# Layer 1 of a two-layer R-GCN: SP loads one tile of the even step row by row, ACT one tile of the odd step

## What is computed

```python
def _rgcn_conv(x, src, dst, edge_type, W_r, W_root, b):
    seg = dst * r + edge_type
    msg = x[src]
    agg = segment_sum(msg, seg, n * r).reshape(n, r, d)
    cnt = segment_sum(ones, seg, n * r).reshape(n, r, 1)
    mean = agg / maximum(cnt, 1.0)
    return einsum('nrd,rdk->nk', mean, W_r) + x @ W_root + b
...
h = maximum(_layernorm(x), 0); x = x + _L0_gnn_ref(h, src, dst)
h = maximum(_layernorm(x), 0)
for l in range(2):
    h = relu(_rgcn_conv(h, ...)) + relu(h @ res_W[l] + res_b[l])
x = x + h
```

## Time and profile before

| | |
|---|---|
| runs | 10280.56, 10290.72, 10291.77 us; median 10290.72 us |
| profiled execution | 10278.55 us, of which the span of its instructions is 10276.7 us |
| layer 1, first to last gather | 2367.31 to 6330.91 us |
| layer 2, first gather | 6362.22 us |
| busy share of the span | POOL 73%, DVE 52%, PE 44%, PE weight loads 32%, ACT 22% |
| mean granted TensorE clock | 0.65 of full speed |

### The profile page before, as it was taken

The page is one execution under the profiler, slowest core; times in us unless marked ns, Lnnn a source line. Parts: engine busy times, 40 slices in busy tenths (PEclk is TensorE's granted clock), DMA queues, the critical chain, the costliest instruction groups (busy, mean ns, idle before and its releaser), DMA issues.

```text
span 10276.7 us, 178961 instructions
## 1 busy us (share of the span) xinstructions
PE 4477.1 (44%) x38502; PEld 3253.0 (32%) x38601; DVE 5355.0 (52%) x19831; ACT 2249.7 (22%) x5858; POOL 7548.9 (73%) x8087
## 2 busy tenths in 40 slices
PE   4488888884444444444444443222222222222222
PEld 3366666662222222222222222222222222222222
DVE  9866666666667767767767765222222222222222
ACT  7855555551111111111111111000000000000000
POOL 6667777766777777777777776777777777777777
PEclk8899999996666666666666666555555555555555
DMA  3244444445444444444444443111111111111112
GB/s 89 63 139 149 147 147 147 148 136 171 146 149 143 145 149 143 145 148 139 149 148 141 147 148 120 30 29 29 29 29 29 29 29 29 29 29 29 29 29 41
DMA packets 534216, 1014.18 MB, mean 99 GB/s; under 512 B 242660, under 2 KB 289268, under 8 KB 532964
## 3 DMA queue, kind: packets, MB, share of 16 engines
q1 hardware_dynamic: 256500, 746.14, 20.0%
q0 software_dynamic: 251296, 259.66, 13.1%
q10 hardware_dynamic: 25872, 2.47, 0.3%
HBM read 557.66 MB, written 454.36 MB: 98 GB/s over the span
## 4 chain that ended last, share of the span: by engine, by line
POOL 64%; issue 24%; PE 5%; DVE 5%; ACT 1%; DMA 1%; POOLq 0%; DVEq 0%; SPq 0%; ACTq 0%
POOL rows L895 35%; POOL w_raw L895 28%; DVE ystage L1643 2%; PE block_ps L1399 1%; PE y_ps L1313 1%; ACT scr L1048 1%; PE y_ps L1391 1%; DVE onehot L1678 1%; PE sums_ps L1364 1%; DVE w_parts L1826 0%; DVE w_room L1826 0%; PE signs_ps L1313 0%; DMA rows<-h_table,idx_st 0%; DMA y_table<-ystage 0%; POOLq L496 0%
## 5 line engine op out<-in xcount | busy, mean ns | idle before, releaser
L895 POOL DMA_INDIRECT rows<-y_table,idx_st x3136 | 2961.6, 944 | 1036.6 <-issue 1036.6
L895 POOL DMA_INDIRECT w_raw<-y_table,idx_st x3163 | 2986.7, 944 | 964.9 <-issue 964.9
L1749 DVE TENSOR_SCALAR rr<-rr 128x64 f32<-128x64 f32 x198 | 41.3, 209 | 4073.5 <-PE block_ps L1341 4073.5
L1510 PE MATMUL sums_ps<-onehot,rows 128*64 128x64 f32 x6468 | 755.2, 313 | 2632.6 <-DMA rows<-y_table,idx_st 2557.9
L1510 PE MATMUL sums_ps<-w_raw 128*64 128x64 f32 x6424 | 751.4, 314 | 2542.0 <-DMA w_raw<-y_table,idx_st 2505.4
L895 POOL DMA_INDIRECT rows<-h_table,idx_st x1386 | 1323.9, 955 | 554.2 <-issue 435.3
L1510 PEld LDWEIGHTS sums_ps<-onehot,rows 128*64 128x64 f32 x6468 | 702.7, 222 | 2712.5 <-DMA rows<-y_table,idx_st 1607.7
L1510 PEld LDWEIGHTS sums_ps<-w_raw 128*64 128x64 f32 x6424 | 704.9, 224 | 2615.7 <-issue 2094.1
L999 ACT ACTIVATE idx_st<-edges 128x11 int32 (+1 forms) x714 | 140.7, 211 | 5545.0 <-PE sums_ps L1510 3061.9
L1688 DVE TENSOR_SCALAR_CACHE_REDUCE w_parts<-edges,step_key 128x384 bf16<-128x384 f32 x1568 | 850.7, 605 | 15.6 <-DVE step_key L1668 15.6
L1292 PE MATMUL y_ps<-scr,hT 128*128 128x512 bf16 (+1 forms) x2574 | 728.3, 428 | 111.7 <-ACT hT L1009 93.7
(11 more groups left out here) (238 smaller groups left out, 7495.9 us busy)
## 6 DMA issues: line engine op xcount, KB each, us to landing
y_table<-ystage SPq DMA_DIRECT2D x396, 768.0 KB
edges<-key_row SPq DMA_DIRECT2D x198, 832.0 KB
rows<-y_table SPq DMA_DIRECT2D x9408, 0.2 KB
y_table<-ystage SPq DMA_DIRECT2D x198, 608.0 KB
w_raw<-y_table ACTq DMA_DIRECT2D x6272, 0.2 KB
w_parts<-key_row SPq DMA_DIRECT2D x99, 832.0 KB
w_raw<-y_table,idx_st POOLq DMA_INDIRECT x3163
rows<-y_table,idx_st POOLq DMA_INDIRECT x3136, 2.5
```

What stands on the lines that cost most here:

```text
L895: pool.indirect_dma_start(out=rows_of(l, u)[:, j, k, 0:D], out_offset=None, in_=table, in_offset=bass.IndirectOffsetOnAxis(ap=idx_of(l, u, ...
L1510: ins = nc.tensor.matmul(sums_ps[u][0:width, c:c + W], rows_of(l, u)[:, j, k, 0:width], onehot_of(l, u)[:, j, k, :], start=False, stop=False)
```

## The change

In layer 1 the odd step's tile 10 is taken from POOL as well. SP now loads the whole tile of the even step, ACT the whole tile of the odd step, each four batches a step. ACT's batches stand where layer 2 has them, so that in layer 1 one lies after each `stage` of the first third, one after each of the three groups of evictions; ACT also loads the row numbers of its own tile and places them at the end of the even step.

```diff
-    ROW_LAYER = 2
-    ACT_ROWS = 32
...
         def by_rows(l, u):
-            return l == ROW_LAYER or l == 1 and u == 0
+            return l >= 1
...
-                    per_step = 32 if l == 1 else ROW_HALF
-                    load_rows(sp, mybir.EngineType.SP, l, 0, 0, 2 * per_step)
+                    load_rows(sp, mybir.EngineType.SP, l, 0, 0, P)
...
                         def next_rows(n):
                             if more:
-                                load_rows(sp, mybir.EngineType.SP, l, 0, u * per_step + n * (per_step // 2), per_step // 2)
+                                load_rows(sp, mybir.EngineType.SP, l, 0, u * ROW_HALF + n * (ROW_HALF // 2), ROW_HALF // 2)
...
-                    if l == 1:
...
-                        wait_alone(act, row_placed[0], loads)
-                        load_rows(act, mybir.EngineType.Activation, l, 0, P - 2 * ACT_ROWS, 2 * ACT_ROWS)
...
+                    load_row_idx(act, 1, 0, 1)
+                    place_rows(1, loads)
+                    wait_alone(act, row_placed[1], loads)
+                    load_rows(act, mybir.EngineType.Activation, l, 1, 0, ROW_HALF)
...
                         def next_rows(n):
-                            if l == ROW_LAYER and (more or u == 0):
+                            if more or u == 0:
                                 load_rows(act, mybir.EngineType.Activation, l, 1,
                                           (1 - u) * ROW_HALF + n * ROW_BATCH, ROW_BATCH)
-
-                        def shared_rows(n):
-                            if l == 1 and more:
-                                load_rows(act, mybir.EngineType.Activation, l, 0,
-                                          P - 2 * ACT_ROWS + u * ACT_ROWS + n * ROW_BATCH, ROW_BATCH)
...
                         if u == 0 and more:
                             place_rows(0, i + loads + 1)
-                            if l == ROW_LAYER:
-                                load_row_idx(act, 1, i + 1, 1)
-                            else:
-                                wait_alone(act, row_placed[0], i + loads + 1)
+                            load_row_idx(act, 1, i + 1, 1)
                         stage_ahead(0)
                         next_rows(0)
-                        shared_rows(0)
...
-                        shared_rows(1)
...
                         next_rows(3)
-                        if l == ROW_LAYER and u == 0 and more:
-                            place_rows(1, i + 2)
-                            wait_alone(act, row_placed[1], i + 2)
+                        if u == 0 and more:
+                            place_rows(1, i + loads + 1)
+                            wait_alone(act, row_placed[1], i + loads + 1)
```

More of the change, by code:

```diff
@@ L430, in gnn_kernel @@
         gathered = [[[sem(f"gathered{l}{u}{j}") for j in range(J)] for u in range(2)] for l in range(3)]
-        rows_landed = [None] + [[sem(f"rows_landed{l}{n}") for n in range(l)] for l in (1, 2)]
+        rows_landed = [None, [sem("rows_landed10"), sums_saved[1]], [sem(f"rows_landed2{n}") for n in range(2)]]
         row_idx_loaded = [sem(f"row_idx_loaded{n}") for n in range(2)]
@@ L1131, in _ @@
                     place_rows(0, loads)
-                    if l == 1:
-                        for slot in range(2):
-                            n = YG * NBK
-                            act.wait_ge(y_saved[l - 1][slot], 16 * ((n + 1 - slot) // 2 + 1))
-                        wait_alone(act, row_placed[0], loads)
-                        load_rows(act, mybir.EngineType.Activation, l, 0, P - 2 * ACT_ROWS, 2 * ACT_ROWS)
-                    if l == ROW_LAYER:
[L1139 to L1145, removed]
+                    for slot in range(2):
+                        n = YG * NBK
+                        act.wait_ge(y_saved[l - 1][slot], 16 * ((n + 1 - slot) // 2 + 1))
+                    load_row_idx(act, 1, 0, 1)
+                    place_rows(1, loads)
+                    wait_alone(act, row_placed[1], loads)
+                    load_rows(act, mybir.EngineType.Activation, l, 1, 0, ROW_HALF)
                     def act_step(i, u, last=False):
```

## The result

The changed kernel took 10618.46 us (median of 4 runs, 10603.67 to 10623.23), the kernel before 10291.24 beside it: a ratio of 1.0318, 95% interval 1.030 to 1.0336, some 327 us slower. The forecast was 10258 us and its range ended at 10380.

A forecast was written before the change was run, and what follows sets the result against it. POOL's gathers were taken to bound layer 1 at 81.2 us a pair; afterwards ACT and SP's 37.6 + 42.4 = 80.0 nearly tied POOL's 79.9, giving -32 us with the layer's ends: 10258 us, range 10222 to 10380.

The forecast's parts named there:

- What bounds the kernel, and what the change removes: POOL's back-to-back gathers, 1.249 us each, bound layer 1; 49 fewer remove 61.2 us, a pair going from 81.2 to 79.9.
- Even to odd, 37.6 us: ACT's loop, even to odd step in layer 1: 30.15 us seen in layer 2 plus 7.4 of evictions.
- the mark: ACT's `stage` of the second third, from which step intervals are measured; step 0 reaches it at 65.9 us.
- Odd to even, 42.4 us: Longer chain through SP, odd to even step in layer 1: 12.9 + 15.9 + 1.15 + 4.56 + 7.86 us.
- SP's jump: Rival, chance 0.09: SP's jump back fetches code, 3.3 us more odd to even, pair 83.3 us, +126 us, 10417 us.
- The landing, 4.56: Odd to even: ACT can place the next pair's row numbers 4.56 us after SP issues their load.
- ACT's own jump back lies under this wait.: Odd to even: ACT's last batch ends at 26.9 us, placing can start at 34.5, so its jump is covered.
- Slow register loads: Rival, chance 0.21: ACT's loads slow while saves and keys move; pair 82.6 us, 92 us longer, 10383 us.
- POOL keeps the bound: Rival, chance 0.23: pair of ACT and SP below 79.4 us; gain 61 us, 10229 us.
- near tie: Likeliest case, chance 0.26: pair of ACT and SP between 79.4 and 80.2 us, -61 to -21 us.
- no change: Rival, chance 0.21: pair of 80.2 to 81.1 us; gain given back at the layer's end.
- The start and the end of the layer.: Layer 1: step 0's mark at 65.9 us, last `hT` copy at 3936.9 after POOL's first gather, today 3969.4.

The follow-up runs named there:

- last rows first: Changed kernel plus early row numbers, shifted SP/ACT loops, groups 0 and 1 evicted together, some PE zero products, even-step last ACT batch before group 2's eviction: 10231.83 us, 0.9954.
- SP's loops elsewhere: Changed kernel with 30 already met waits on SP ahead of layer 1, so SP's loops lie at another place of the program: ratio 1.0250.
- the numbers early: Changed kernel, but in layer 1 SP loads the even tile's row numbers a pair ahead: 10445 us, ratio 1.0162.
- ACT's part alone: Changed kernel, but only ACT's odd-step tile is loaded by ACT; the even step's tile comes from POOL, SP loads no rows in layer 1: ratio 1.0223.

## Why the prediction was wrong, point by point

What failed is the sum for the loops of ACT and SP: 80.0 us a pair were forecast, 87.4 measured, 4.0 too little from even to odd and 3.4 from odd to even.

**What bounds the kernel, and what the change removes.** Right: a layer of 64 gathers a pair takes 80.0 us a pair (64 x 1.250, forecast 79.9) when nothing holds POOL, shown by the last rows first kernel.

**Even to odd, 37.6 us: a sum of terms that were too small.** Measured 41.6. Group 0, 4.1, took 4.6 (PE's clock); each batch with the group behind it, 8.2 and 8.1, took 9.6 and 9.3; the rest, from the last batch to the mark, 18.1 instead of 17.2. I had taken a batch from layer 2, where SP saves nothing, and an eviction from a stream in which PE runs ahead. A batch put between two evictions changes both: it runs into the save that the eviction released, and PE runs out of banks and, waiting, falls to 1.2 GHz (0.50 in the stretch of group 0 shown above). I named the batch that is longer beside the saves as what would make me wrong above all; I did not price it.

**Odd to even, 42.4 us: SP's jump, counted as cheap.** Measured 45.8. Group 1 ended 1.9 us later for the reasons above, and SP's save and batches behind it, 15.9, took 0.3 more. "The save of group 2, the jump back and the load of the next pair's row numbers", 1.15 us, took 4.8, +3.6: the rival that I gave 0.09. The landing, 4.56, took 2.4 on average, -2.2, because the jump had let the save drain; the kernel with SP's loops elsewhere shows both at once. These four terms, and -0.1 from placing to mark, make the 3.4, within 0.1.

**"ACT's own jump back lies under this wait."** True as far as the wait was there, and it hid that ACT's own chain was nearly as long: with the numbers early the wait is gone, and odd to even is still 42.6, with a jump of 2.5 on ACT (42.9 with ACT's part alone, where that jump is 4.0). So removing the wait altogether gave 3.4 us a pair, and not the 6.7 that break-even needed.

**The rivals.** Slow register loads: fell, the medians are 1.2 us. SP's jump: right on the price, 3.3 us forecast and 3.6 found, with the landing as a rebate. My reason against it, that SP's jump in layer 2 with as many rows was cheap, was a reason of one place in a program: in the changed kernel the same loop of layer 2 costs some 2.5 us a jump. The Trainium skill (Runtime: NRT & Kernel Launch, section Instruction fetch mechanics) says that a taken branch out of the two blocks held forces a fetch. The trace agrees, with 1085 packets against 147. What decides here is where the loop lies in the program, which I left out; how the blocks lie no run shows. POOL keeps the bound, near tie, no change: all needed a pair under 81.1.

**The start and the end of the layer.** The first mark, forecast 65.9 us after POOL's first gather, came at 2433.58 - 2365.57 = 68.0. ACT's copy of `hT` in the last step, forecast at 3936.9, came at 6658.61 - 2365.57 = 4293.0: the 48 pairs, 7.4 us longer each, make nearly all of the 356 us between.

## What to carry to other kernels

A step that only fills idle time of an engine is not free when it stands between two operations of a chain: price it in its new neighbourhood (what its predecessor releases on other queues, how far the next engine can run ahead, what clock it has after waiting), and add up each engine's loop on its own before asking which one covers the other. Small transfers that somebody waits for go ahead of the operation that releases a large one. When a loop grows, look at the first instruction behind its jump, and try it a few dozen instructions further on in the program.

## What the runs showed of the hardware that I had not expected

- The cost of a jump back hangs on where the loop lies: SP's loop of layer 2, with the same instructions, jumped in 0.23 us before, in 2.4 to 2.7 in the changed kernel, and in 0.3 with 30 waits ahead of it. The numbers 30 and 55 came from a guess (pieces of 128 instructions, three of them free); they fitted four loops, which does not prove the guess.
- Issuing a row took ACT 0.21 us, but up to 0.94 shortly after SP had issued a save of 768 KB, with no row load on SP's queue (the kernel with ACT's part alone). In the changed kernel, from 2450 to 6200 us, 179 of ACT's 5490 issues took over 0.6 us, and 174 of them started within 2 us of a save's issue.
- Rows of 256 bytes that ACT issued moved no packet for 5.6 us while a save of 608 KB from SP's queue was in transfer; 7.5 us instead of 3.8 until PE could use the last.
- Useless products on PE made the kernel faster: granted clock 0.82 instead of 0.65 between 4400 and 4600 us, 2.5 us a pair.
